# A graph network on one Trainium2 core: node update by pairs of blocks, and part of the edge-row scatter moved into the first attention loop

## What is computed

```python
# layer 0, after the messages of each edge are formed
agg   = segment_sum(m, dst)                 # m = relu(...) @ eW2 + eb2, summed per node
h_upd = relu([h, agg] @ nW1 + nb1) @ nW2 + nb2
x     = x + layer_norm(h + h_upd) * gamma + beta
# layer 1: attention over edges, needs only the type of an edge (edge_type_64)
# layer 2: attention over edges, needs the 64 features of an edge (edge_attr_64)
# layer 3: graph attention and gates
```

## Time and profile before

| | us |
|---|---|
| median of 3 runs (lowest to highest) | 4753.07 (4742.81 to 4775.06) |
| the profiled execution, its own time | 4752.21 |
| its span from first to last instruction | 4750.4 |
| DVE busy in it | 3232.1 (68%) |
| POOL busy in it | 3258.8 (69%) |
| PE busy in it | 2720.6 (57%) |
| mean granted clock of TensorE | 0.772 of full speed |

### The profile page before, as it was taken

The page is one execution under the profiler, slowest core; times in us unless marked ns, Lnnn a source line. Parts: engine busy times, 40 slices in busy tenths (PEclk is TensorE's granted clock), DMA queues, the critical chain, the costliest instruction groups (busy, mean ns, idle before and its releaser), DMA issues. The chain is left out here.

```text
span 4750.4 us, 53808 instructions
## 1 busy us (share of the span) xinstructions
PE 2720.6 (57%) x11404; PEld 1443.0 (30%) x11404; DVE 3232.1 (68%) x7318; ACT 763.4 (16%) x2124; POOL 3258.8 (69%) x2932
## 2 busy tenths in 40 slices
PE   4235778888886936466666566577878742000005
PEld 4234322222225933233333233233444321000003
DVE  7597378888882134599999833588888885566652
ACT  0020100000001212233333211011111112000006
POOL 0586777777775786677777486677777736777742
PEclk8555899999997968788888758788788866555559
DMA  3235356666663223566666323556666633444430
GB/s 148 53 87 162 83 162 176 176 174 173 170 171 54 46 35 82 136 178 179 169 171 170 96 35 85 135 165 168 169 167 168 166 85 94 105 105 105 105 69 27
DMA packets 408512, 594.23 MB, mean 125 GB/s; under 512 B 266756, under 2 KB 273032, under 8 KB 407410
## 3 DMA queue, kind: packets, MB, share of 16 engines
q0 software_dynamic: 185552, 519.27, 40.2%
q1 hardware_dynamic: 222882, 74.01, 6.8%
HBM read 532.97 MB, written 59.26 MB: 125 GB/s over the span
## 5 line engine op out<-in xcount | busy, mean ns | idle before, releaser
L1147 POOL DMA_INDIRECT edge_ring<-tab,edge_rec x480 | 505.3, 1053 | 146.2 <-issue 129.8
L1885 POOL DMA_INDIRECT state<-tab,edge_rec x480 | 470.4, 980 | 154.9 <-issue 145.9
L1593 PE MATMUL edge_psX<-edge_w_edge,edge_featT 64*128 64x256 f32 x1920 | 442.0, 454 | 234.7 <-DVE edge_prod L1658 232.1
L1598 PE MATMUL edge_psX<-state,ident 128*128 128x512 f32 x720 | 468.5, 786 | 151.5 <-DMA state<-tab,edge_feat 140.0
L1536 POOL DMA_INDIRECT state<-tab,edge_rec x360 | 408.1, 1134 | 141.0 <-issue 109.7
L1536 POOL DMA_INDIRECT state<-tab,edge_feat x360 | 389.9, 1083 | 109.7 <-issue 103.9
L1593 PEld LDWEIGHTS edge_psX<-edge_w_edge,edge_featT 64*128 64x128 f32 x1920 | 298.9, 218 | 515.0 <-issue 431.2
L1176 PE MATMUL edge_psX<-state,ident 128*128 x720 | 378.1, 635 | 131.0 <-DVE edge_ring L1204 130.8
L2058 PE MATMUL gate_psW<-ident,gate_w_nat 128*128 128x128 f32 x12 | 2.8, 426 | 650.2 <-DMA gate_w_nat<-in_L_gnn_W_ih 650.2
L1209 DVE SCALAR_TENSOR_TENSOR state<-edge_ring,state 128x512 f32 x480 | 337.9, 704 | 30.8 <-DVE edge_ring L1204 18.5
L1204 DVE TENSOR_TENSOR edge_ring<-edge_psX,edge_ring 128x1024 f32<-128x1024 f32 x240 | 293.9, 1225 | 84.0 <-PE edge_psX L1183 51.7
(11 more groups left out here) (392 smaller groups left out, 6116.2 us busy)
## 6 DMA issues: line engine op xcount, KB each, us to landing
sorted_d<-state SPq DMA_DIRECT2D x7, 2380.0 KB
state<-src_rows SPq DMA_DIRECT2D x25, 562.5 KB
state<-low_rows SPq DMA_DIRECT2D x25, 562.5 KB
state<-tab,edge_rec POOLq DMA_INDIRECT x840, 3.6
edge_ring<-tab,edge_rec POOLq DMA_INDIRECT x600, 3.6
update_row_out<-in_edge_attr SPq DMA_DIRECT2D x40, 156.2 KB
edge_rec<-rec_d SPq DMA_DIRECT2D x364, 8.0 KB, 2.7
state<-tab,edge_feat POOLq DMA_INDIRECT x360, 3.7
```

Of the source, the lines that this page charges most:

```text
L1147: pool.indirect_dma_start(out=ring[:, k, s, :], out_offset=None, in_=S["tab0"][:, :], in_offset=bass.IndirectOffsetOnAxis(ap=rec[:, k, R_S ...
L1593: pe.matmul(psX[k % 2][:, s % 2, s // 2, :], featT[lo:lo + ED, k % 4, s // PAIR, :], w_edge[lo:lo + ED, :], start=(s < 2), stop=False, ski ...
L1598: last = pe.matmul(psX[k % 2][:, a, :, :], S["ident"][:, :], ring[k % RING].rearrange("p (c a) f -> p a c f", a=2)[:, a, :, 0:D], start=Fa ...
L1885: pool.indirect_dma_start(out=ring[:, k, s, :], out_offset=None, in_=S["tab3"][:, :], in_offset=bass.IndirectOffsetOnAxis(ap=rec[:, k, R_S ...
```

## The change

`update_nodes` handles blocks in 13 pairs (the last has one block): transposes read `S["big"]` and `S["H"]` directly, so DVE's staging copies are gone; the products by `eW2` and `nW1` have 256 columns; the bias `nb2` becomes one more product with one row for each block (L1400 of the changed file), and the statistics of a block are taken right after its result. The loops over blocks are written out. `RowScatter` gets a ring size of its own. The 85 groups are shared out anew: 10 in `make_tables` 0, 24 in `update_nodes` (ring of 2), 8 in `make_tables` 1, 24 in `attend` 1 (new: two groups in each of the first 12 turns, ring of 2), 11 in `project_out`, 8 in `make_tables` 2. In `make_tables` all scatters but 25 are issued ahead of the first block, and one after each block.

```diff
-ROW_TURNS = EDGE_C // (HERE * ROW_RING)
+ROW_TURNS = 12
+TURN_GROUPS = 2
+UPDATE_GROUPS = 24
+TURNS_MIN = -(-(-(-N_EDGES // (QE * P))) // AQ)
...
+    def __init__(self, ph, S, A, first, groups, ring=ROW_RING):
...
+    def load_group(self, sp, k, g):
+        at = bass.ds((g + self.first) * HERE, HERE)
+        sp.dma_start(self.row[:, k, :, 0:ED], self.features[:, at, :]).then_inc(self.loaded[k], 16)
+        sp.dma_start(self.row[:, k, :, ED].bitcast(I32), self.S["dst_i"][:, at], allow_slow_non_contiguous=True).then_inc(self.loaded[k], 16)
+        sp.dma_start(self.idx[:, k, :], self.S["place_i"][:, at]).then_inc(self.loaded[k], 16)
+
     def load(self, sp):
         sp.wait_ge(self.cleared, 1)
...
+        for g in range(self.groups):
+            k = g % self.ring
+            if g >= self.ring:
+                sp.wait_ge(self.stored[k], g // self.ring * (16 * HERE))
+            self.load_group(sp, k, g)
...
-        ROWS_AT, ROWS_N = ((0, 2), (10, 2), (15, 2), (0, 0))[layer]
+        ROWS_AT, ROWS_N = ((0, 10), (34, 8), (77, 8), (0, 0))[layer]
...
+                if scattered:
+                    scattered.some(pool, 0, ROWS_N * HERE - NB)
                 for b in range(NB):
...
                     if scattered:
-                        scattered.some(pool, b * ROWS_N, ROWS_N)
+                        scattered.some(pool, ROWS_N * HERE - NB + b, 1)
...
-        scattered = RowScatter(ph, S, A, 2, 8)
+        scattered = RowScatter(ph, S, A, 10, UPDATE_GROUPS, 2)
...
+                def aggregate(i):
+                    b0, n = PAIRS[i]
+                    pe.wait_ge(s_sT, i + 1)
+                    if i:
+                        pe.wait_ge(s_mT, i)
                     for f in range(2):
...
+                            pe.matmul(psM[:, f, 0:n, :], eW2[:, c, f * P:(f + 1) * P], sumsT[:, c, 0:n, :], start=(c == 0), stop=False)
+                        last = pe.matmul(psM[:, f, 0:n, :], eb2[:, f, :], deg_row[:, b0:b0 + n, :], start=False, stop=True)
...
+                def down(i):
+                    n = PAIRS[i][1]
+                    pe.wait_ge(s_uT, i + 1)
+                    if i:
+                        pe.wait_ge(s_y, i)
+                    for k in range(n):
+                        for c in range(4):
+                            pe.matmul(psY[:, k, :], upT[:, c, k, :], nW2[:, c, :], start=(c == 0), stop=False)
+                        last = pe.matmul(psY[:, k, :], S["ones"][0:1, :], rows[0:1, 0, :], start=False, stop=True)
                     last.then_inc(s_Y, 1)
...
-                dve.wait_ge(s_y, NB + 1)
-                step(dve.tensor_tensor(Y, Y, bc(rows[:, 0, :], 1, [P, NB, D]), ALU.add))
-                for b in range(NB):
-                    last = block_stats(dve, F, b)
+                for i, (b0, n) in enumerate(PAIRS):
+                    dve.wait_ge(s_Y, i + 1)
+                    dve.tensor_tensor(Y[:, b0:b0 + n, :], psY[:, 0:n, :], S["H"][:, b0:b0 + n, :], ALU.add).then_inc(s_y, 1)
+                    dve.wait_ge(s_y, i + 1)
+                    for k in range(n):
+                        last = block_stats(dve, F, b0 + k)
...
+        scattered = RowScatter(ph, S, A, 42, ROW_TURNS * TURN_GROUPS, TURN_GROUPS) if layer == 1 else None
...
+                if layer == 1:
+                    sp.wait_ge(scattered.cleared, 1)
+                    with nc.Fori(0, ROW_TURNS, engines=[sp.engine], hint_back_edge=True) as t:
+                        for g in range(TURN_GROUPS):
+                            hold(sp, scattered.stored[g], t * (16 * HERE))
+                            scattered.load_group(sp, g, t * TURN_GROUPS + g)
+                        for q in range(AQ):
+                            load(t, q, t * AQ + q)
...
+                if layer == 1:
+                    with nc.Fori(0, ROW_TURNS, engines=[pool.engine], hint_back_edge=True) as t:
+                        for q in range(AQ):
+                            rows(t, q)
+                            for i in range(TURN_GROUPS * HERE * q // AQ, TURN_GROUPS * HERE * (q + 1) // AQ):
+                                if i % HERE == 0:
+                                    hold(pool, scattered.loaded[i // HERE], (t + 1) * 48)
+                                scattered.one(pool, i // HERE, i % HERE)
...
-        scattered = RowScatter(ph, S, A, 12, 3)
+        scattered = RowScatter(ph, S, A, 66, 11)
```

More of the change, by code:

```diff
@@ L748 @@
 class RowScatter:
[L753 to L758, removed]
+    def __init__(self, ph, S, A, first, groups, ring=ROW_RING):
+        self.S, self.first, self.groups, self.ring = S, first, groups, ring
+        self.row = ph.sb("row_out", [EDGE_P, ring, HERE, SROW])
+        self.idx = ph.sb("row_idx", [EDGE_P, ring, HERE], I32)
+        self.loaded = [ph.sem(f"row_loaded{k}") for k in range(ring)]
+        self.stored = [ph.sem(f"row_stored_{k}") for k in range(ring)]
         self.cleared = ph.sem("rows_cleared")
@@ L778, in one @@
             in_=self.row[:, k, j, :], in_offset=None).then_inc(self.stored[k], 16)
[L780 to L785, removed]
     def some(self, pool, begin, count):
-        for i in range(begin, min(begin + count, self.turns * ROW_RING * HERE)):
-            t, k, j = i // (ROW_RING * HERE), i // HERE % ROW_RING, i % HERE
+        for i in range(begin, begin + count):
+            g, j = i // HERE, i % HERE
             if j == 0:
-                pool.wait_ge(self.loaded[k], (t + 1) * 48)
-            self.one(pool, k, j)
+                pool.wait_ge(self.loaded[g % self.ring], (g // self.ring + 1) * 48)
+            self.one(pool, g % self.ring, j)
     def finish(self, pool):
-        for k in range(ROW_RING):
-            pool.wait_ge(self.stored[k], self.turns * HERE * 16)
+        for k in range(self.ring):
+            pool.wait_ge(self.stored[k], len(range(k, self.groups, self.ring)) * HERE * 16)
 def shared(nc, ctx):
@@ L1322, in _ @@
                 add_beta(pool, S, F)
-                scattered.scatter(pool)
+                scattered.some(pool, 0, UPDATE_GROUPS * HERE)
                 scattered.finish(pool)
@@ L1360, in _ @@
             def _(pe):
-                def turn(b):
-                    if not isinstance(b, int) or b:
-                        pe.wait_ge(s_hT, b)
-                    pe.wait_ge(s_st, b + 1)
-                    for c in range(4):
-                        pe.transpose(psR[:, c * P:(c + 1) * P], sums[:, c * P:(c + 1) * P], S["ident"][:, :])
-                    for c in range(2):
-                        last = pe.transpose(psH[:, c * P:(c + 1) * P], hst[:, c * P:(c + 1) * P], S["ident"][:, :])
-                    last.then_inc(s_T, 1)
@@ L1397, in _ @@
                 turn(0)
[L1398 to L1409 removed]
+                for i in range(LAST + 1):
+                    aggregate(i)
+                    if i < LAST:
+                        turn(i + 1)
+                    if i:
+                        down(i - 1)
+                    up(i)
+                down(LAST)
             @block.vector
@@ L1631, in _ @@
                 pre = Chain(dve, s_v)
+                if layer == 1:
+                    scattered.clear(dve)
                 dve.wait_ge(s_w, 32 if layer == 2 else 32 * heads)
@@ L1720, in _ @@
                 add_beta(pool, S, F)
-                scattered.scatter(pool)
+                scattered.some(pool, 0, 11 * HERE)
                 scattered.finish(pool)
```

160 lines of the change are left out of this document (65 added, 95 removed).

## The result

The changed kernel takes 4841.7 us in the median of four runs (4820.4 to 4859.2), the kernel before 4753.2 in the same comparison: a ratio of 1.0171, 95% interval 1.0143 to 1.0198. It is slower by 88 us by the medians and by 81 by the ratio; 4814 was forecast, 62 more. The profiled execution took 4820.4 us, 68 more than that of before, and is the fastest of its four.

What follows compares the result with a forecast made beforehand. DVE was taken to bound attend 1, POOL nearly full there, and POOL to bound attend 2 and end update_nodes, make_tables 1 and project_out. 4752.2 - 162.1 + 220.1 + 3.7 = 4813.9 us; range 4715 to 4880.

Steps and rivals of the forecast that it cites:

- two large terms: attend 1: POOL's turn 61.5 us instead of 50.3, plus 7.8 us idle at 11 turn boundaries (85.8); together +220.1.
- The start, 3.7: Start of attend 1: SP passes two row groups ahead of the first record, +3.7 us, bounds 0 to 7.4.
- make_tables and project_out: Fewer or earlier scatters on POOL: make_tables 1 -23.4 us, make_tables 2 -23, project_out -32.3, ending with DVE.
- the 7.8 a group allowed for it: update_nodes: with a ring of two, reload waits make a group of five scatters 7.8 us instead of 7.4.
- the term that was mis-sized: update_nodes, ended by PE and DVE instead of POOL: -83.4 us, range -60 to -90.
- the one-row products ... about zero: update_nodes: one-row products halved in psM and two added in psY, net about zero per pair.
- Idle at the turn's end is covered: Rival, attend 1: records arrive in time, so the 86 us of idle vanish; 4728 us, chance 0.12.
- POOL has room: Rival, attend 1: scatters cost only issue time, a turn is 54.8 us; 4648 us, chance 0.10.
- longer idle: Rival, attend 1: a reload queues behind gathers in the DMA engines, +4 us a turn; 4858 us, chance 0.14.
- pairs cost: Rival, update_nodes: ACT's copies for two blocks become waits, 2 us a pair; 4839 us, chance 0.12.
- wide products are cheap: Rival, update_nodes: wide-pass columns cost half of narrow ones, saving 5.4 us a pair; 4768 us, chance 0.03.
- full blocking: Rival, attend 1: DVE's two-input operations stretch some five transfers a quad, +317 us; 5131 us, chance 0.03.

Runs made afterwards that it cites:

- old_shares: Changed kernel with the earlier share-out of groups (40 in update_nodes, none in attend 1): 4732.0 us, 0.9968; on the slow chip 5377.7 us, 0.9791.
- rec_first: Changed kernel with only SP's order in attend 1 changed, second row group loaded ahead of record 4 instead of record 0: 4744.5 us, 0.999.
- no_rows: Changed kernel without the loads and scatters of rows in attend 1: 4606.2 us, 0.9699.
- narrow: Changed kernel with the old update_nodes (one block at a time, 128 columns) but the new number of scatters, ring of two: 4849.7 us, 1.0214.
- bias_dve: `rec_first` with update_nodes' bias nb2 added by DVE instead of PE's one-row products: 4720.1 us, 0.9939; on the slow chip 5400.0 us, 0.9836.
- one_group: Changed kernel shared out 10, 33, 8, 13, 12, 9, one group in each of 13 turns of attend 1: 4693.3 us, 0.988.
- one_input: `rec_first` with five two-input DVE operations per quad of attend 1 reading one input: 4676.0 us, 0.9847; on the slow chip 5427.5 us, 0.9913.
- fitted: `one_group` shared out 10, 31, 9, 13, 11, 11, ending update_nodes' and project_out's queues earlier: 4688.2 us, 0.9872; on the slow chip 5380.8 us, 0.981.

## Why the prediction was right

**What bounds.** DVE's idle times of the earlier trace rows were POOL's, as read: they went with the scatters, and came back in `old_shares` (65.8 and 32.7 us). One thing in POOL's queue was read too simply: its 200 scatters did not all go at 1.48 us. Two were held, for 7.38 and 15.13 us (last section). Neither enters the sum, since the 120 that are left end before DVE's closing operations.

**attend 1** was right in its two large terms. POOL's work for a turn, 61.5 us from `attend` 2's pace, measured 61.5 where nothing else disturbs (`rec_first`); the idle time at the head, 7.8 beyond POOL's pace, measured 7.8 (8.09 less 0.30). It is made of the steps that were named, 3.25, 3.6 and 2.43 us for 3.0, 3.7 and 2.6, and it went when SP's order was turned. The start, 3.7, was too small: POOL idles 25.2 us before the stage's first gather, against 18.9 in `no_rows`. That the stage with `make_tables` 1 came to +201.0 against +200.4 is closer than its terms are.

**make_tables and project_out**: -23.3 (seen alone in `no_rows`), -21.6 and -31.2 for -23.4, -23 and -32.3. (The rows named for the first of them add up to 23.1.) The ring of two never waited: 120 scatters ran from 1475.85 to 1652.37, at 1.483 each; the 7.8 a group allowed for it was not needed.

**update_nodes** is the term that was mis-sized, -74.5 for -83.4. The part of it that is the smaller queue measured 53.3 (`narrow`), 53.8 by the forecast's rows. The new code measured 21 instead of 29.7. Against `narrow`, the way to PE's first transposes is 11.0 us shorter (10.3 forecast) and the tail 14.7 (14.4), but the loop between them is 4.5 longer where 5 shorter was forecast. The step that failed is "the one-row products ... about zero": they make a pair 1.2 us longer, psY's two costing 1.64 (`bias_dve`) and psM's saving 0.4. The wider products and the transposes together save 0.7, somewhat more than the 0.43 forecast. So a pair is 0.54 longer than two blocks instead of 0.43 shorter.

**The rivals.** "Idle at the turn's end is covered" and "POOL has room" are refuted by the rows of [8.09 <-DMA edge_rec<-rec_d] and by the turn of 61.5 without idle; "longer idle" by 7.92 to 8.29 (and its landing of 17.1 us in the earlier trace rows was no slow transfer: it is that of the scatter of the earlier trace rows which POOL held for 15.45, so 1.6 us behind its end); "pairs cost" has a sign that is right and a mechanism that is not (PE's own products, no wait for ACT), and its 4839 mixes two counts, as 2 us a pair are 24 more and from -5 to +24 are 29; "wide products are cheap" by the pair of 18.36; "full blocking", with which a turn would be 96 us, by 69.

**The total.** The profiled execution is 68 us slower than that of before, 62 by the forecast. That it is so near is in part luck: the stages that were forecast sum to 74, and `attend` 2 happened to be 8 shorter. By the ratio the kernel is 81 us slower, 19 more than forecast, and `update_nodes` accounts for 9 of them. The median is 21 us above that execution. In `narrow`, whose profiled execution is at its median, ten turns have a mean of 69.5 us against 69.0 there, 6 us in all, and `attend` 2 is 5 longer; what else varies between executions is not settled.

## What to carry to other kernels

Work moved into the gaps of another engine's stage is paid by the turn, not by the average: count all transfers of a turn at the pace of a stage that is already full on that engine, and look in the issuing queue for what stands behind the new wait. A load that waits for the end of a turn must not stand ahead of the loads that open the next one; half a turn later it cost nothing here. A queue that runs on the side is best ended before the main engine's closing operations begin, which took 27 us off two stages here. A product with a single row is not free: its passes took 0.31 us where those with 128 rows took 0.23.

## What the runs showed of the hardware

**A held scatter outlasts single operations.** In the kernel before, POOL's scatters at the end of `update_nodes` lie beside DVE's rows:

```profile
1706.38 7.38 POOL L776 DMA_INDIRECT sorted_d<-update_row_out,update_row_idx  x1 [0.30 <-issue]
1715.54 1.17 POOL L776 DMA_INDIRECT sorted_d<-update_row_out,update_row_idx  x1 [0.30 <-issue]
1727.44 15.13 POOL L776 DMA_INDIRECT sorted_d<-update_row_out,update_row_idx  x1 [0.30 <-issue]
```

The first starts beside the addition of 6.83 us with two inputs and ends 1.05 us after it. The second, like its neighbours, is not held beside the statistics, 25 operations of one input in 8.26 us. The third lies beside the closing chain of operations with two inputs. The 14.45 us in `one_group` lie beside the same chain, some forty operations of 0.41 us back to back, of which these are the first and the last rows:

```profile
1711.66 0.84 DVE L1269 TENSOR_TENSOR state<-state,update_rows 128x256 f32<-128x256 f32 x2 [0.74 <-ACT state L1252]
1727.85 0.74 DVE L1272 TENSOR_TENSOR state<-state 128x256 f32<-128x256 f32 x2
```

The Trainium skill ("SBUF — State Buffer", "SBUF: two separate sides") speaks of a lock for the whole instruction. The scatter of 7.38 us agrees with that. The one of 14.45 us ends 1.06 us after the whole chain, so it got no turn between the chain's operations. It is not the chain alone that decides: the scatters at 1711.90 and 1713.44 ran beside its first operations in 1.24 and 1.45 us. Why those passed and the next did not is not shown, and no run changed the chain. In `attend` 1 of `rec_first`, where such operations stand between others, the longest gather takes 2.01 us where the median is 0.99; in `one_input` the longest takes 1.46.

**A chip on which PE stalls.** On the chip where the kernel before takes 5490 us, PE in the written-out `update_nodes` of `old_shares` reads:

```profile
1889.19 1.12 PE L1399 MATMUL update_psY<-update_nW,update_upT 128*128 128x256 f32 x4 [0.23 <-issue]
1890.62 1.13 PE L1399 MATMUL update_psY<-update_nW,update_upT 128*128 128x256 f32 x4 [0.31 <-issue]
1892.06 0.59 PE L1400 MATMUL update_psY<-update_rows,ones 1*128 1x256 f32 x2 [0.31 <-issue]
...
1893.75 0.59 PE L1388 MATMUL update_psU<-update_hT,update_nW 128*128 128x256 f32 x2 [0.25 <-issue]
```

Between groups of two to four instructions PE idles for 0.2 to 0.3 us with nothing that the profile shows as its reason; the first ten pairs took 22.8 to 33.5 us instead of 18.4, and the stage lasted 372 us with DVE last; in `one_input`, with 120 scatters, they took 14.8 to 25.0, in `bias_dve` 11.3 to 32.2 and in `fitted` 18.4 to 23.8. The cause is open, and the loop of the kernel before was not profiled on that chip, so it isn't shown that written-out code has a part in it. Most of what that chip adds lies elsewhere: of the 655 us by which the profiled `old_shares` is longer there, 192 lie before the first `make_tables`, 156 from there to `update_nodes`, and 20 in `update_nodes`. The ratios there (0.979 to 0.991) have the sign of those on the other chips for all four kernels.
